# Adding the first experts' rows and the normalisation's factors inside the attention's stage, beside its first two batches

## What is computed

```python
h = _L0_tok_ref(x, L0_tok_W, L0_tok_b)
h = h + _L0_attn_ref(_layernorm(h, axis=-1), ...)
h = h + _L0_ffn_ref(_layernorm(h, axis=-1), ...)     # 8 experts, top 1
h = h + _L1_attn_ref(_layernorm(h, axis=-1), ...)    # 8 heads of 16, relative positions
h = h + _L1_ffn_ref(_layernorm(h, axis=-1), ...)     # 64 experts, top 2, and a shared one
return h
```

```python
attn1 = jnp.einsum('bhqd,bhkd->bhqk', rq, rk)
attn2 = jnp.einsum('bhqd,qkd->bhqk', rq, rk2)      # keys by distance, clipped at 68
attn = jax.nn.softmax((attn1 + attn2) * (1.0 / math.sqrt(c)), axis=-1)
w1 = jnp.einsum('bhqk,bhkd->bhqd', attn, rv)
w2 = jnp.einsum('bhqk,qkd->bhqd', attn, rv2)       # values by distance
out = (w1 + w2).transpose(0, 2, 1, 3).reshape(b, t, c)
return out @ Wo + bo
```

## Time and profile before

| | us |
|---|---|
| median of 3 runs | 2062.87 |
| the profiled execution's own time | 2057.68 |
| its span in the trace | 2055.9 |
| TensorE busy | 1715.7 (83% of the span) |
| VectorE busy | 1438.6 (70%) |
| ScalarE busy | 928.4 (45%) |
| GpSimd busy | 828.1 (40%) |

### The profile page before, as it was taken

The page is one execution under the profiler, slowest core; times in us unless marked ns, Lnnn a source line. Parts: engine busy times, 40 slices in busy tenths (PEclk is TensorE's granted clock), DMA queues, the critical chain, the costliest instruction groups (busy, mean ns, idle before and its releaser), DMA issues. The chain is left out here.

```text
span 2055.9 us, 59079 instructions
## 1 busy us (share of the span) xinstructions
PE 1715.7 (83%) x21927; PEld 1411.4 (69%) x21927; DVE 1438.6 (70%) x3464; ACT 928.4 (45%) x2319; POOL 828.1 (40%) x1677
## 2 busy tenths in 40 slices
PE   4999999999888856991599999999999999857640
PEld 3888888888667746991477777777777777634420
DVE  5777777777668854665477888888888888644323
ACT  2211111121177614771366766667667666414320
POOL 2333333333014664661002443434444444447771
PEclk9999999999999967996699999999999999979875
DMA  8900000000040012222133333333333333335537
GB/s 300 133 0 0 0 0 0 0 0 0 1 174 14 30 35 59 70 72 90 32 58 63 77 73 71 70 72 73 73 75 79 74 75 72 89 114 151 154 99 253
DMA packets 312955, 147.80 MB, mean 72 GB/s; under 512 B 205142, under 2 KB 291572, under 8 KB 312308
## 3 DMA queue, kind: packets, MB, share of 16 engines
q1 hardware_dynamic: 300164, 118.58, 24.8%
q0 software_dynamic: 12544, 25.91, 3.9%
HBM read 72.23 MB, written 73.37 MB: 71 GB/s over the span
## 5 line engine op out<-in xcount | busy, mean ns | idle before, releaser
L1939 ACT ACTIVATE rel_e<-rel_s_ps,rel_neg_max 128x255 f32<-128x255 f32 x512 | 199.9, 479 | 47.8 <-DVE rel_neg_max L2192 47.1
L2192 DVE TENSOR_REDUCE rel_neg_max<-rel_s_ps 128x4 f32<-128x1020 f32 x128 | 156.2, 1221 | 91.7 <-PE rel_s_ps L1684 88.9
L524 PE MATMUL tok_main_ps<-tok_w_h,tok_feat_h 128*128 128x512 f32 x512 | 204.6, 400 | 0.9 <-DVE tok_feat_low L99 0.9
L524 PE MATMUL tok_main_ps<-tok_w_h,tok_feat_l 128*128 128x512 f32 x512 | 200.1, 391 | 0.0
L524 PE MATMUL tok_main_ps<-tok_w_l,tok_feat_h 128*128 128x512 f32 x512 | 199.8, 390 | 0.0
L84 POOL TENSOR_TENSOR tok_q_pre<-tok_v_q,tok_v 128x128 f32 (+1 forms) x32 | 38.8, 1214 | 306.0 <-DVE tok_q L273 291.7
L1705 PEld LDWEIGHTS rel_t_ps<-all_k_ident,rel_e 128*128 128x128 f32 x1024 | 110.5, 142 | 70.0 <-issue 64.7
L1668 PE MATMUL rel_s_ps<-rel_k_h,rel_q_head_h 128*128 128x256 f32 x512 | 156.7, 306 | 0.0
L1705 PE MATMUL rel_t_ps<-all_k_ident,rel_e 128*128 128x128 f32 x1024 | 139.7, 280 | 16.5 <-issue 11.7
L1668 PE MATMUL rel_s_ps<-rel_k_l,rel_q_head_h 128*128 128x256 f32 x512 | 146.2, 285 | 0.0
L1668 PE MATMUL rel_s_ps<-rel_k_h,rel_q_head_l 128*128 128x256 f32 x512 | 146.1, 285 | 0.0
(11 more groups left out here) (374 smaller groups left out, 4633.9 us busy)
## 6 DMA issues: line engine op xcount, KB each, us to landing
rel_q_rep<-q_rows SPq DMA_DIRECT2D x256, 64.0 KB
o_rows<-rel_rv SPq DMA_DIRECT2D x256, 64.0 KB
x_slots<-early_zeros SPq DMA_DIRECT2D x16, 520.0 KB, 6.5
exp_x<-x_slots SPq DMA_DIRECT2D x32, 260.0 KB
y_rows<-early_zeros SPq DMA_DIRECT2D x16, 512.0 KB, 6.5
final_y<-y_rows SPq DMA_DIRECT2D x16, 512.0 KB, 10.3
exp_x<-x_slots SPq DMA_DIRECT2D x72, 65.0 KB, 1.9
rows_y<-y_rows SPq DMA_DIRECT2D x8, 512.0 KB, 6.9
```

What stands on the lines that cost most here:

```text
L524: nc.tensor.matmul(main_ps[s][:, cols], feat[fk][:, s, j, :], w_p[wk][:, j, cols], start=(j == 0 and (fk, wk) == (0, 0)), stop=False)
L1939: last = nc.scalar.activation(e[u % 2][:, n, 0:L], s_ps[u % 2][:, n, 0:L], ACT.Exp, bias=neg_max[u % 2][:, n:n + 1])
L2192: nc.vector.tensor_reduce(neg_max[u % 2][:], s_ps[u % 2][:, :, 0:L], AX.X, ALU.max, negate=True)\
```

## The change

`add_rows` and the call of `norm_factors(..., "norm2")` go. What they did is done inside `relative_attention`, and the stages have changed as follows.

- `experts_top1`: VectorE prepares the attention's tables at the end of its list (`attention_tables`): the scaling of the query's bias, the two subtractions and the addition.
- SyncE issues the eight chunk loads first in the attention's stage. The chunks land in buffers that the attention only needs later (`eT`, `rv`, `x1`).
- VectorE adds chunk 0, takes its statistics, and computes mean and rstd of these eight tiles (batches 0 to 3) in a chain of small instructions with ScalarE's square root; ScalarE then runs one Exp on a single column.
- GpSimd, after its memsets, adds chunks 1 to 7 (`rows_added`). VectorE takes their statistics one chunk at a time (`stats_of_rows`), spread over its head and the slots 1 and 2 of batch 0.
- GpSimd then computes mean and rstd of the other 56 tiles (`norm_rest`, with three Newton steps in place of the square root); VectorE waits for it before it normalises batch 4.
- The head is reordered: TensorE computes batch 0's first scores before batch 1's query and value projections; of batch 1 the remainders of the last three groups go to slot (0, 0), its position queries to slot (0, 1); the first maximum and the first exponentials come earlier in their engines' lists.

The diff, cut to its core:

```diff
+                def attention_tables():
+
+                    attention.wait(dve)
+                    bq, bv, vends, vtab = (attention.sb[n] for n in ("bq", "bv", "value_ends", "value_table"))
+                    nc.vector.tensor_scalar(bq[:], bq[:], 1.0 / float(D) ** 0.5, None, ALU.mult)
+                    ends = vends[:, :, 0:HD]
+                    for t, lo in ((1, 0), (0, 2 * P)):
+                        nc.vector.tensor_tensor(vtab[:, lo:lo + P, :], vtab[:, lo:lo + P, :],
+                                                ends[:, t:t + 1, :].to_broadcast([P, P, HD]), ALU.subtract)\
+                            .then_inc(table_ready, 1)
+                    dve.wait_ge(table_ready, 2)
+                    nc.vector.tensor_tensor(vends[:], vends[:], bv[:].unsqueeze(1).to_broadcast([P, 2, D]), ALU.add)
+
                 run(step, 3)
+                attention_tables()
...
+        y_at = [b[:].rearrange(dims)[:, k * CH * D:(k + 1) * CH * D].rearrange("p (n d) -> p n d", d=D)
+                for b, dims, k in ((eT[0], "p t n k -> p (t n k)", 0), (eT[0], "p t n k -> p (t n k)", 1),
+                                   (eT[1], "p t n k -> p (t n k)", 0), (eT[1], "p t n k -> p (t n k)", 1),
+                                   (rv, "p t n k -> p (t n k)", 0), (x1[0], "p t n k -> p (t n k)", 0),
+                                   (x1[1], "p t n k -> p (t n k)", 0), (x1[2], "p t n k -> p (t n k)", 0))]
...
+                for c in range(NCH):
+                    sp.dma_start(y_at[c], y0_rows[0:ROWS0, :].rearrange("(p n) d -> p n d", p=P)[:, c * CH:(c + 1) * CH, :])\
+                        .then_inc(y_in[c], 16)
                 repeat_queries(0, 0)
                 repeat_queries(1, 1)
...
                     weights.wait(pe)
-                    for b in range(2):
-                        turn_x(b)
-                        project_k(b)
-                        project_q(b)
-                        project_v(b)
-                    for u in range(2):
-                        content(0, u, 0)
-                        position_scores(0, u, 0)
+                    turn_x(0)
+                    project_k(0)
+                    project_q(0)
+                    project_v(0)
+                    turn_x(1)
+                    project_k(1)
+                    content(0, 0, 0)
+                    project_q(1)
+                    project_v(1)
+                    position_scores(0, 0, 0)
+                    content(0, 1, 0)
+                    position_scores(0, 1, 0)
 
...
-                    act.wait_ge(ready, 3)
-                    act.wait_ge(zeroed, 4)
+                    act.wait_ge(var_ready, 1)
+                    nc.scalar.activation(var_f[:], var_f[:], ACT.Sqrt).then_inc(std_ready, 1)
+                    nc.scalar.activation(warm[:], K["ident"][:, 0:1], ACT.Exp)
                     for b in range(2):
                         read_x(b)
                         read_k(b, b)
                         read_q(b)
-                        round_queries(b, b, range(4))
+                        if b == 0:
+                            act.wait_ge(zeroed, 4)
+                        round_queries(b, b, range(4) if b == 0 else (0,))
                     exps(0, 0)
+                    round_queries(1, 1, (1, 2, 3))
+                    act.wait_ge(rows_added, NCH - 1)
 
...
+                for c in range(1, NCH):
+                    pool.wait_ge(y_in[c], 16)
+                    hc = h[:, c * CH:(c + 1) * CH, :]
+                    nc.gpsimd.tensor_tensor(hc, hc, y_at[c], ALU.add).then_inc(rows_added, 1)
+
+                def norm_rest():
+
+                    mean_e, m2_e, mean_o, m2_o = (stats[:, CH:NT, k] for k in (1, 2, 4, 5))
+                    pool.wait_ge(rows_stats, NCH)
...
+                    link(nc.gpsimd.tensor_scalar(root_r[:].bitcast(I32), var_r[:].bitcast(I32), -0.5, float(0x5f3759df),
+                                                 ALU.mult, ALU.add))
+                    for k in range(3):
+                        link(nc.gpsimd.tensor_tensor(newton_r[:], root_r[:], root_r[:], ALU.mult))
+                        link(nc.gpsimd.tensor_tensor(newton_r[:], newton_r[:], var_r[:], ALU.mult))
+                        link(nc.gpsimd.tensor_scalar(newton_r[:], newton_r[:], -0.5, 1.5, ALU.mult, ALU.add))
+                        step = nc.gpsimd.tensor_tensor(root_r[:] if k < 2 else rstd[:, CH:NT], root_r[:], newton_r[:],
+                                                       ALU.mult)
+                        if k < 2:
+                            link(step)
+                        else:
+                            step.then_inc(norm_ready, 1)
+
+                norm_rest()
                 link(nc.gpsimd.memset(tick[:], 0.0))
...
+                def stats_of_rows(c):
+                    if c > 0:
+                        dve.wait_ge(rows_added, c)
+                    for n in range(c * CH, (c + 1) * CH):
+                        last = nc.vector.bn_stats(one_tile(stats, n), one_tile(h, n))
+                    last.then_inc(rows_stats, 1)
+
+                def first_rows():
+
+                    hc, first = h[:, 0:CH, :], Chain(dve, first_fac)
+                    dve.wait_ge(y_in[0], 16)
+                    nc.vector.tensor_tensor(hc, hc, y_at[0], ALU.add).then_inc(first_added, 1)
+                    dve.wait_ge(first_added, 1)
+                    stats_of_rows(0)
+                    dve.wait_ge(rows_stats, 1)
+                    mean_e, m2_e, mean_o, m2_o = (stats[:, 0:CH, k] for k in (1, 2, 4, 5))
+                    first(nc.vector.tensor_tensor(spread_f[:], mean_e, mean_o, ALU.subtract))
+                    first(nc.vector.scalar_tensor_tensor(spread_f[:], spread_f[:], 0.25, spread_f[:],
+                                                         ALU.mult, ALU.mult))
+                    first(nc.vector.tensor_tensor(var_f[:], m2_e, m2_o, ALU.add))
+                    first(nc.vector.scalar_tensor_tensor(var_f[:], var_f[:], 1.0 / D, spread_f[:],
+                                                         ALU.mult, ALU.add))
+                    nc.vector.tensor_scalar(var_f[:], var_f[:], EPS, None, ALU.add).then_inc(var_ready, 1)
+                    first(nc.vector.tensor_tensor(mean[:, 0:CH], mean_e, mean_o, ALU.add))
+                    first(nc.vector.tensor_scalar(mean[:, 0:CH], mean[:, 0:CH], 0.5, None, ALU.mult))
+                    dve.wait_ge(std_ready, 1)
+                    first(nc.vector.reciprocal(rstd[:, 0:CH], var_f[:]))
+
                 def read_x(b):
                     if after(b, 1):
                         dve.wait_ge(xT_done, b)
+                    if 2 * b == CH:
+                        dve.wait_ge(norm_ready, 1)
                     normalise(nc, x[:, 0, :], h, mean, rstd, 2 * b)
                     normalise(nc, x[:, 1, :], h, mean, rstd, 2 * b + 1).then_inc(x_ready, 1)
...
-                        if have(b + 1) and after(b, 1):
+                        if have(b + 1):
                             queries_remainder(b + 1, 1 - r, (1, 2, 3))
...
-                        if have(b + 1) and after(b, 1):
+                        if have(b + 1):
                             position_queries(b + 1, 1 - r)
...
+                    if b == 0 and u in (1, 2):
+                        stats_of_rows(NCH - 3 + u)
...
-                    nc.vector.tensor_scalar(bq_scaled[:], bq_sb[:], SCALE, None, ALU.mult)
-                    ends = vends_sb[:, :, 0:HD]
-                    for t, lo in ((1, 0), (0, 2 * P)):
-                        nc.vector.tensor_tensor(vtab[:, lo:lo + P, :], vtab[:, lo:lo + P, :],
-                                                ends[:, t:t + 1, :].to_broadcast([P, P, HD]), ALU.subtract)\
-                            .then_inc(ready, 1)
-                    dve.wait_ge(ready, 2)
-                    nc.vector.tensor_tensor(vends_sb[:], vends_sb[:], bv_sb[:].unsqueeze(1).to_broadcast([P, 2, D]),
-                                            ALU.add).then_inc(ready, 1)
-                    dve.wait_ge(ready, 3)
-                    for b in range(2):
-                        read_x(b)
-                        keys_remainder(b, b)
-                        queries_remainder(b, b, range(4))
-                        if b == 0:
-                            read_v(0, 0)
+                    first_rows()
+                    read_x(0)
+                    stats_of_rows(1)
+                    stats_of_rows(2)
+                    keys_remainder(0, 0)
+                    read_x(1)
+                    stats_of_rows(3)
+                    read_v(0, 0)
+                    queries_remainder(0, 0, range(4))
+                    keys_remainder(1, 1)
+                    stats_of_rows(4)
                     position_queries(0, 0)
-                    position_queries(1, 1)
+                    stats_of_rows(5)
+                    maxima(0, 0)
+                    queries_remainder(1, 1, (0,))
                     read_x(2)
```

(9 more changed lines are left out.)

52 lines of the change are left out of this document (20 added, 32 removed).

## The result

The kernel after takes **2037.32 us** (median of 4 runs, 2034.47 to 2041.06), where the kernel before took 2062.76 beside it: 0.9888 of the time, interval 0.9871 to 0.9906, 25.4 us less. The profiled execution of after took 2041.06 us (span 2039.2), against 2057.68 (span 2055.9) of before.

What follows compares the result with a forecast made beforehand. The prediction took the attention's delayed start as the bound: TensorE does nothing for 46 us, from 935 to 981. Gains of 18.1 + 13.9 - 0.5 - 0.5 = 31.0 us took the median 2062.87 to 2031.9, forecast 2032, range 2021 to 2041.

Steps and rivals of the forecast that it cites:

- rival B: Six waits on adds, low clock through the first slots, scatter held up 2.3: gain 23, 2040 us; 0.22 together with Rival C.
- Rival C: Adds end ahead of the head, VectorE's in-order statistics waiting for each: gain 24.4, 2038.5 us; 0.22 together with rival B.
- the sum: Whole change: 18.1 at TensorE's start plus 13.9 in the head, less 0.5 and 0.5, gives 31.0 us.
- Tables, leak 0.5: End of experts' stage: moved table subtractions may delay GpSimd's last scatter, bounds 0 to 2.3 us, 0.5 taken as loss.
- The 9.3 us of cover: Gap from the last scatter's issue to the next stage's loads, to hide VectorE's tables, which would otherwise cost 5.1 us.
- Waits in the chain: Batch 0's factors and normalisation: small VectorE instructions wait for whole GpSimd adds of 2.4 us, 4 to 6, five taken.
- the 18.1 forecast: Attention's opening: batch 0's first TensorE instruction starts at 963.4 in place of 981.53, 18.1 us earlier.
- The head, 13.9: From batch 0's first TensorE instruction to the third maximum: reordering makes it 25.0 us where it was 38.9, gaining 13.9.
- clock 0.5: Head and first slots: low TensorE clock into the first scores, full after; 0.5 us deducted for a relapse.
- The slots: Batch 0's slots: moved remainders and statistics fit VectorE's idle time, costing nothing; if the third failed, some 0.3 us.
- Rival A: Factors: small instructions pass GpSimd's adds; landmark moves 29.0, head 12.5, less 1: 40.5 us, 2022.4; chance 0.2.
- Rival D: Attention's slots: TensorE's clock stays at half, slots of 6.0 us take about 10; 2080 us with 12 slots; chance 0.01.

Runs made afterwards that it cites:

- after_again: The kernel after, unchanged, measured again beside the other kernels: 2033.4 us, 0.9844 of before's 2066.0.
- after_third: The kernel after, unchanged, measured once more on a chip where all kernels take longer: 2176.6 us, 0.9859 of before's 2205.8.
- before_again: The kernel before, unchanged, profiled again on a chip where all kernels take longer: 2205.5 us, 1.0003 of before's 2205.8.
- only_head: Against the kernel after: row adds and 64-column factors back in stages of their own; moved tables and reordered head kept. 2195.1 us, 0.993 of before's 2209.6.
- adds_after_x0: Against the kernel after: GpSimd begins its seven adds only when batch 0 is normalised. 2174.4 us, 0.9839 of before's 2209.6.
- best_dve: Against the kernel after: all adds on VectorE, tables behind the last scatter's landing, chunks' work respread. 2022.2 us, 0.9793 of before's 2066.0.
- best_warm: Against best_dve: eight unused 256-column matmuls on TensorE while it waits for batch 0's normalisation. 2024.6 us, 0.9811 of before's 2066.0.

## Why the prediction was right, and which terms were off

The forecast was 2032 in 2021 to 2041, and the median is 2037.3: inside the range, but above the 2027 to 2036 that had the chance of 0.55, where B and C had 0.22. The medians of after differ from before's by 25.4, 32.6 and 29.2 us where the sum said 31.0. The mechanisms of the chain and of the head were right; the tables' term was wrong in mechanism and size. The kernel lies between the forecast and rival B, which named the three things that went against it.

At the third maximum the traces show 25.1 us of the 31.0, so 5.9 are missing: 4.6 ahead of TensorE's start and 1.3 in the head.

- **Tables, leak 0.5 of a range of 0 to 2.3: wrong, and outside the range.** It is 3.55. I argued that only the scatter's reading of operands was open to VectorE, and took at most one subtraction. The trace shows two waits: first the one-column tick ahead of the scatter, an instruction that I had not counted, waits for the first subtraction (2.15), then the scatter's issue for the second (2.85). The 9.3 us of cover hid VectorE's work, as said, but not what that work holds up.
- **Stage opening: not in the sum.** Another 0.4: I let the loads start at the same point, and overlooked that the enclosing `Bench` now closes ahead of them.
- **Waits in the chain, five taken of 4 to 6: right in kind.** Six in after and after_again, five in after_third; adds at 2.31 for the 2.4 taken from the earlier trace rows. From the loads to TensorE's start 21.1 us for the 19.9 of the forecast. With the late opening (4.0, of which 0.5 foreseen) that is the whole distance between the 18.1 forecast less 0.5 and the 13.0 found: 3.5 + 1.2 = 4.7 against 4.6.
- **The head, 13.9: right.** 12.1 in after, 13.7 in after_again, 14.5 in after_third against before_again (25.0 for 39.5), 13.8 in only_head. What is short in after is the clock: position scores of 1.95 for 1.10 and a last part of the head at the half clock, where I had let the full one come with the value projection. The row that gave the 1.10 lay in before's only full-clock stretch up to there, 1001.7 to 1005.1 (1.00 in a window of 1001.75 to 1005); after it the clock changed three times more and stayed full only from 1018.8. From the first transposes to those of the exponentials 21.4 for 19.8. The term "clock 0.5" should have been up to 2. (The head's parts of 2.6, 1.2, 0.5, 0.6 and 1.10 add up to 6.0, not 6.1.)
- **The slots:** statistics cost little in them (5.87 and 5.15 for 6.02 and 5.15; 6.25 and 5.16 in after_again), and batch 4 waits for no factor: GpSimd's 21 instructions end at 1020.3, and the normalisation of batch 4 begins at 1032.7. 1.6 us are lost later, open.
- **Rival A** (small instructions pass the adds) falls with adds_after_x0: 12.0 us lie in those waits. That best_dve ends near what it gave (2022.4) is chance in part: best_dve gets there with other edits, and against a before of 2066.0 (43.8 us, where A had 40.5).
- **Rival C** is half right: six of the seven adds are over (974.4) when TensorE's first instruction starts (974.59), and the time is near what it gave. But not by its mechanism: VectorE's statistics of chunks 1 and 2 wait for nothing (they follow the normalisation at 974.36). It is the factors' chain that waits for the adds.
- **Rival D** did not come: the clock was 1.00 from 1000 to 1021.

## What to carry to other kernels

Work that is moved under another engine's wait is free only if nothing that the wait depends on contends with it: look at what the other engine still has to issue, down to a one-column tick, and count up to one whole instruction of yours for each. Elementwise work with two inputs that is given to GpSimd "to relieve VectorE" cost twice here: 2.31 for 1.22 us, and in a chain of small VectorE instructions beside it each link that contends paid about one add (0.17 became 2.2); statistics and a reciprocal did not. Compare two traces from a landmark just ahead of the change, and take the gain from medians on one chip: here the profiles alone said 16.6 us, the landmarks 25, the medians 25 to 33.

## What was unexpected of the hardware

- A VectorE subtraction with two SBUF inputs also holds up the issue of an indirect DMA by GpSimd: 2.85 us for 0.98, and back at 0.98 when the subtraction is moved away.
- In best_warm TensorE's clock rose 0.9 us before 6.4 us of matmuls ended, and fell again unused: 0.86 in a stretch with 0.40 of 4 us busy, then 0.50 for most of the head. It came back later than without the warming (40.2 for 33.2 us behind the landmark).
- One and the same kernel starts TensorE 2.3 us apart (35.5 and 33.1), by whether one instruction begins 0.04 us ahead of an add or behind it.
